# A vision-transformer block on one core, rewritten: loads by partition rows, 16-wide scores, biases off the matmuls, folded low-rank factors, halves in turn

## What is computed

```
h  = patches @ W.T + b + pos_emb                      # 512x768 @ 768x256
z  = layernorm(h);  k, q, v = split(z @ W_kqv + b_kqv)  # 256 -> 3x256, 16 heads of 16
a  = softmax(q k^T / 4 + slope_h * (j - i), causal)     # within one image: 16x16 per head
h  = h + (a v) @ W_proj + b_proj
z2 = layernorm(h)
f  = z2 @ (tern(w_fc)*s).T + gate * (z2 @ v.T @ fast_b.T @ u.T)   # 256 -> 1024, rank 16
h  = h + (relu(f)**2) @ (tern(w_mlp)*s2).T            # 1024 -> 256
# s: mean |w| of a row; tern: w/s rounded and clipped to -1, 0, 1
```

## Time and profile before

| | |
|---|---|
| median of 3 runs | 98.38 us (98.31 to 99.17) |
| the profiled execution | 99.0 us, span 97.2 us |
| PE / PEld busy | 71.5 / 57.4 us |
| DVE / ACT / POOL busy | 58.7 / 43.4 / 19.7 us |
| mean granted TensorE clock | 0.895 |

### The profile page before, as it was taken

One profiled execution on the slowest core, in us unless ns is written; L12 is line 12 of the kernel. 1 busy time (PEld: TensorE's weight loads), 2 busy tenths in 40 slices (PEclk: granted clock), 3 DMA queues, 4 the chain that ended last, 5 costly groups with the idle time before them and its releaser, 6 DMA issues.

```text
span 97.2 us, 1915 instructions
## 1 busy us (share of the span) xinstructions
PE 71.5 (74%) x776; PEld 57.4 (59%) x776; DVE 58.7 (60%) x118; ACT 43.4 (45%) x86; POOL 19.7 (20%) x21
## 2 busy tenths in 40 slices
PE   5958589899999999440000258696699999999980
PEld 4725467777777787330000247674577887888970
DVE  0300037957289799999999500228873867885590
ACT  3503003599762670619100087350223994976600
POOL 6000024089990000000199600000000000000000
PEclk9999999999999999997555555559999999999999
DMA  1899999970000000000000000000000000000015
GB/s 52 239 287 263 312 380 384 396 195 12 0 0 0 0 7 7 0 0 0 0 0 0 0 0 7 7 0 0 0 7 0 0 0 0 7 0 0 0 40 176
DMA packets 7644, 6.75 MB, mean 69 GB/s; under 512 B 2002, under 2 KB 7378, under 8 KB 7636
## 3 DMA queue, kind: packets, MB, share of 16 engines
q1 hardware_dynamic: 7056, 6.25, 19.9%
q10 hardware_dynamic: 580, 0.38, 1.7%
HBM read 6.10 MB, written 0.52 MB: 68 GB/s over the span
## 4 chain that ended last, share of the span: by engine, by line
PE 45%; DVE 23%; DMA 11%; POOL 7%; ACT 6%; issue 4%; SPq 1%; ACTq 0%; DVEq 0%
PE psum L327 14%; PE psum L488 9%; PE psum L457 8%; DMA pos_sb<-pos 8%; POOL mlp_tern L1069 6%; PE psum L415 4%; PE psum L467 3%; DMA wtok_sb<-wtok_t 3%; PE psum L340 3%; DVE shifted L913 3%; DVE smax L911 2%; ACT mlp_t L675 2%; DVE bn L851 2%; PE psum L331 2%; DVE h L849 2%
## 5 line engine op out<-in xcount | busy, mean ns | idle before, releaser
L331 PE MATMUL psum<-wtok_sb,x_sb 128*128 128x256 f32 x48 | 11.6, 388 | 3.0 <-DMA wtok_sb<-wtok_t 2.7
L331 PEld LDWEIGHTS psum<-wtok_sb,x_sb 128*128 128x128 f32 x48 | 8.6, 190 | 5.5 <-DMA wtok_sb<-wtok_t 3.7
L517 PE MATMUL psum<-ident_bf,mlp_tern 128*128 128x128 bf16 x16 | 1.9, 312 | 12.7 <-DVE mlp_tern L816 12.7
L1069 POOL TENSOR_SCALAR mlp_tern<-mlp_sb,mlp_scale 128x1024 bf16<-128x1024 f32 x2 | 5.7, 2843 | 18.9 <-DVE mlp_scale L805 18.9
L517 PEld LDWEIGHTS psum<-ident_bf,mlp_tern 128*128 128x128 bf16 x16 | 1.6, 146 | 12.9 <-DVE mlp_tern L816 12.9
L457 PE MATMUL psum<-zt_hi,fc_t 128*128 128x256 f32 x32 | 8.4, 296 | 0.0
L488 PE MATMUL psum<-sq_hi,mlp_t 128*128 128x256 f32 x32 | 8.4, 298 | 0.0
L999 DVE TENSOR_TENSOR kqv_sb<-wtok_sb 128x512 f32<-128x512 f32 x8 | 5.5, 690 | 4.7 <-PE psum L488 2.8
L457 PE MATMUL psum<-zt_lo,fc_t 128*128 128x256 f32 x32 | 7.9, 281 | 0.0
L774 ACT ACTIVATE wtok_sb<-psum,fc_scale 128x256 f32<-128x256 f32 x16 | 6.7, 468 | 2.8 <-PE psum L467 2.8
L488 PE MATMUL psum<-sq_lo,mlp_t 128*128 128x256 f32 x32 | 7.8, 281 | 0.0
(11 more groups left out here) (117 smaller groups left out, 179.0 us busy)
## 6 DMA issues: line engine op xcount, KB each, us to landing
fc_sb<-w_fc SPq DMA_DIRECT2D x1, 1024.0 KB, 11.6
mlp_sb<-w_mlp SPq DMA_DIRECT2D x1, 1024.0 KB, 8.2
x_sb<-x_t SPq DMA_DIRECT2D x2, 384.0 KB, 8.9
kqv_sb<-w_kqv SPq DMA_DIRECT2D x3, 256.0 KB, 9.5
x_sb<-x_t SPq DMA_DIRECT2D x2, 256.0 KB, 3.7
wtok_sb<-wtok_t SPq DMA_DIRECT2D x2, 256.0 KB, 5.6
out_t<-x_sb SPq DMA_DIRECT2D x4, 128.0 KB, 1.8
x_sb<-x_t SPq DMA_DIRECT2D x2, 128.0 KB, 2.4
```

The source lines that it names most:

```text
L331: return pe.matmul(tok_ps[b], x_sb[:, k, b * P:(b + 1) * P], wtok_sb[:, k, :], start=k == 0, stop=k == KF - 1)
L1069: pool.tensor_scalar(dst[:, m, :], w[:, m, :], scale[:, 2, m:m + 1], None, ALU.is_lt).then_inc(signal, 1)
```

## The change

Most of the file is rewritten. What is computed stays the same, and the last part (`hidden_main`, `hidden_low`, `mlp_out`, `squares`) keeps its products. The parts:

1. Every array is laid out by partition on the host. x and W of one 128-row chunk come as one load with 2 KB per partition (`head`), the second half of x as two loads (`tail`); positions and token bias come in one load from the SP queue, ahead of chunk 4. `fc` and `mlp` come in two loads each. All loads go through SP.
2. The bias of q, k and v is no longer a product. q's is added while it is copied out, k's in its copy, v's by POOL after a DVE transpose.
3. The scores of one image are 16 wide. q is spread with the mask into four copies (`q_spread`, 64 stationary columns) and k moves 16 columns. Softmax tiles have 512 elements per half; `prob_n` is written into a zeroed 32-wide tile so that the 32x32 transpose can be used.
4. v is computed feature-major and transposed by DVE; `values` keeps its number of products.
5. The low-rank path: `fast_b` is folded into u once, v is repeated, and `low_rank_c` with its copy is gone.
6. The fc threshold marks move from DVE to POOL. The order on each engine is new: scores of a half come right behind its q, k, v; softmax of half 0 comes ahead of the fc ternary weights; `values(0)` comes after `turn_fc`, and the mlp ternary weights and `turn_mlp` come after the second layer norm, inside the hidden layer. Standard deviations are taken per block.

```diff
 # SP
-for i, (k, n) in enumerate(CHUNKS): ... x_sb chunk; wtok_sb chunk
+for k in range(KF):
+    if k == LAST:
+        sp.dma_start(pos_sb[:, :, :], pos).then_inc(pos_in, 16)
+    sp.dma_start(head_sb[:, k, :], head[:, k, :]).then_inc(head_in[k], 16)
+# then tail 0, consts, tail 1, w_q, w_k, w_v, w_fc x2, proj_bias, u, v, fb, w_mlp x2, w_proj
 # PE
-    pairs = [(bias_parts[:, c:c + P], ones[:, :])]
+            mm = pe.matmul(ps[f][:, g * HT:(g + 1) * HT], w, part[f][:, k, :], ...)
 ...
-mm = pe.matmul(s_ps[f][j * PAIR:(j + 1) * PAIR, c:c + P],
-               q_sb[rows_, f, g, n * PAIR:(n + 1) * PAIR], k_spread[rows_, f, g, n, :, :], ...)
+for g in range(GRP):
+    for n in range(IMG_H):                      # 16 images of a half
+        t = slice(n * S, (n + 1) * S); c = (g * IMG_H + n) * S
+        for r in range(2):
+            rows = slice(r * 64, (r + 1) * 64)
+            mm = pe.matmul(s_ps[f][rows, c:c + S], q_spread[rows, f, g * IMG_H + n, :, :],
+                           k_sb[rows, f, g, t], start=False, stop=True, ...)
 ...
+for i in range(QUAD):
+    rows = slice(i * PAIR, (i + 1) * PAIR)
+    mm = pe.matmul(y_ps[f][g][rows, n * 64:(n + 1) * 64], v_turned[rows, f, g, n, :],
+                   prob_t[rows, f, 2 * p:2 * p + 2, :], start=True, stop=True)
 # PE order behind the embedding
+query(0); key(0); turn(1, z); value(0); scores(0)
+query(1); key(1); value(1); scores(1)
+fold_u(); turn_fc(); values(0); turn_u(); project(0); values(1)
+turn(0, z2); project(1); low_rank(0); hidden_main(0, 0); hidden_main(0, 1)
+hidden_low(0, 0); hidden_low(0, 1); turn_mlp(); turn(0, h2); hidden(0, 2)
+turn(1, z2); turn(1, h2); hidden(0, 3); mlp_out(0, 0); low_rank(1); mlp_out(0, 1)
+hidden(1, 0); mlp_out(0, 2); hidden(1, 1); mlp_out(0, 3); hidden(1, 2); mlp_out(1, 0)
+hidden(1, 3); mlp_out(1, 1); mlp_out(1, 2); mlp_out(1, 3)
 # ACT order
+norm_std 0, 1; weight_high(Q); zt_hi(0); weight_high(K); norm_std 2, 3; weight_high(V)
+Exp table; query_spread(0); zt_hi(1); fc_sums; query_spread(1); exponentials(0)
+mlp_sums; exponentials(1); Sqrt table; fc_t x2; odd_rows(0); u_t x2; norm_std 0, 1
+odd_rows(1); z2t_hi(0); norm_std 2; low_high(0); norm_std 3; squares(0), (1); mlp_t x2; ...
 # DVE order
+stats1(0), (1); normalise1(0), (1); bias_tables; stats1(2); zt_low(0); normalise1(2)
+stats1(3); normalise1(3); query_spread(0); key_copy(0); zt_low(1); value_turn(0)
+softmax_shift(0); query_spread(1); key_copy(1); softmax_divide(0); scales(fc)
+value_turn(1); softmax_shift(1); low_rank_factors; fc_ternaries; softmax_divide(1)
+rows_sum(0); scales(mlp); stats2(0), (1); normalise2(0), (1); rows_sum(1); z2t_low(0)
+stats2(2), (3); normalise2(2); low_low(0); normalise2(3); mlp ternary x2; squares ...
 # DVE, one of the two spreads of q
+dve.wait_ge(q_spread_act, f + 1)
+dve.scalar_tensor_tensor(q_spread[:, f, :, h, :], src, quad_mask[:, h:h + 1], bias, ALU.mult, ALU.add)
 # POOL order
+memset prob_n; posb; kqv_lo x3; residual(0); value_bias(0); residual(1); below(fc) x8
+value_bias(1); hidden_factors; value_factors; below(mlp) x2
```

More of the change, by code:

```diff
@@ L129, in build_program @@
[L129 to L142, removed]
@@ L163, in build_program @@
[L163 to L174, removed]
+        q_ps = [bank[6], bank[2]]
@@ L179, in build_program @@
-        bias_in = sem("bias_in")
+        fc_in = [sem(f"fc_in{i}") for i in range(2)]
+        mlp_in = [sem(f"mlp_in{i}") for i in range(KE)]
         small_in = sem("small_in")
@@ L421, in project @@
-            def project(f, blocks=range(BH)):
-                pe.wait_ge(proj_in, 16)
-                pe.wait_ge(yt_ready, f + 1)
-                for b in blocks:
-                    split_product(o_ps[f * BH + b], [(yt[:, f, g * BH + b, :], proj_sb[:, g, :])
-                                                     for g in range(GRP)]).then_inc(o_done, 1)
-            def low_rank_a(f):
-                pe.wait_ge(v_split, 2)
+                        mm = pe.matmul(o_ps[f * BH + b], yt[:, f, g, b * P:(b + 1) * P], proj_sb[:, g, :],
+                                       start=g == 0, stop=g == GRP - 1)
@@ new lines, in project, with fold_u, turn_u @@
+                    mm.then_inc(o_done, 1)
+            def fold_u():
+                pe.wait_ge(small_in, 48)
+                for m in range(KH):
+                    mm = pe.matmul(uf_ps[:, m * RANK:(m + 1) * RANK], u_sb[:, m * P:(m + 1) * P], fb_sb[:, :],
+                                   start=True, stop=True)
+                mm.then_inc(uf_done, 1)
+            def turn_u():
+                pe.wait_ge(u_step, 6)
+                for i in range(2):
+                    pe.wait_ge(fct_ready, i + 1)
+                    for m in range(4):
+                        mm = pe.transpose(ut_ps[i][:, m * P:(m + 1) * P],
+                                          u_fold[:, 4 * i + m, :, :, :, :].bitcast(F32), ident)
+                    mm.then_inc(ut_turned, 1)
@@ new lines, in turn_fc, with turn_mlp @@
+            def turn_fc():
+                pe.wait_ge(identbf_done, 1)
+                pe.wait_ge(fc_ternary, KH)
+                for k in range(KE):
+                    for m in range(KH):
+                        mm = pe.transpose(fct_ps[k][:, m * P:(m + 1) * P], fc_tern[:, m, k * P:(k + 1) * P],
+                                          ident_bf[:, :])
+                    mm.then_inc(fct_turned, 1)
+            def turn_mlp():
+                pe.wait_ge(mlp_ternary, KE)
+                for i in range(2):
+                    for m in range(4):
+                        for o in range(KE):
+                            c = (m * KE + o) * P
+                            mm = pe.transpose(mlpt_ps[i][:, c:c + P],
+                                              mlp_tern[:, o, (4 * i + m) * P:(4 * i + m + 1) * P], ident_bf[:, :])
+                    mm.then_inc(mlpt_turned, 1)
@@ L1005, in _ @@
+            scales(fc_sum, fc_scale, KH, E, fc_summed, fc_scaled)
+            value_turn(1)
+            softmax_shift(1)
+            low_rank_factors()
+            fc_ternaries(range(0, KH))
+            softmax_divide(1)
+            rows_sum(0)
+            scales(mlp_sum, mlp_scale, KE, HID, mlp_summed, mlp_scaled)
+            stats2(0)
+            stats2(1)
+            normalise2(0)
+            normalise2(1)
+            rows_sum(1)
+            z2t_low(0)
+            stats2(2)
             stats2(3)
-            normalise(1, 1, h2, std2, rstd2, z2_ready)
+            normalise2(2)
@@ L1007, in _ @@
             low_low(0)
+            normalise2(3)
+            ternary(mlp_sb, mlp_scale, mlp_tern, 0, mlp_cmp, mlp_ternary)
+            ternary(mlp_sb, mlp_scale, mlp_tern, 1, mlp_cmp, mlp_ternary)
             squares(0)
+            squares(1)
+            squares(2)
             z2t_low(1)
-            squares(1)
-            low_a_copy(1)
-            squares(2)
+            squares(3)
             low_low(1)
-            squares(3)
-            for n in range(PAIRS, HALVES * PAIRS):
+            for n in range(STEPS, HALVES * STEPS):
```

1004 lines of the change are left out of this document (472 added, 532 removed).

## The result

The changed kernel takes **93.96 us** (median of four runs, 93.16 to 94.5) against 98.78 us for the kernel before in the same comparison (98.31 to 99.24). The ratio is 0.9506, with a 95% interval of 0.941 to 0.9601: faster, as forecast, but by 4.8 us and not by the 13.4 that lie between the forecast of 85.0 and the 98.4 us that it starts from. The measured time is above the range of 81 to 91.

The account below looks back on a forecast made before the run. Bound by when the last, PE-bound stage can start and its length: `low_rank(0)` at 54.2 instead of 71.08 us, plus 26.6, last product at 80.8, 2.8 behind it, span 83.6, so 85 us; range 81 to 91.

Parts of the forecast that it names:

- The wait for `mlp_tern`: In the hidden layer, PE idles 2.2 us because DVE finishes the mlp ternaries only at 59.7 us.
- the last stage: From `low_rank(0)` to the last product: 23.3 us as before, plus 2.2 idle and 1.1 for `turn_mlp`, 26.6 us.
- The rival in which small matmuls lose their concurrency: Scores and values: row groups sharing one bank run singly at 58 ns, 21 us more, 106 us; chance 0.05.
- q, k, v, scores: Stage after the embedding: scores of a half take 2.4 us, those of half 1 end at 34.7 instead of 39.1 us.
- score instructions at 18 ns: Sign the forecast is right: each of a half's 128 score instructions on PE takes 18 ns.
- scores over 5 us: Sign the forecast is wrong: a run of score or values instructions on PE takes over 5 us.
- the clock stays low: Rival: between 42 us and the hidden layer PE's clock holds at 1.2 GHz, +4 us, 89 us; chance 0.2.
- POOL's marks run at a quarter of 2.84 us each: fc threshold marks on POOL: eight at 0.71 us, 5.7 us in all, from 35.7 to 41.4 us.
- Both ends meet: fc weights: POOL's marks end at 41.4 and DVE's ternaries at 41.7 us, so moving the marks costs PE nothing.
- The first add: DVE's first add in the embedding comes at 8.8 us instead of 13.73; past 10.5 would show the forecast wrong.
- the 13.7 us that it sets against 512 x 27 ns: Gain that lost concurrency of small matmuls would eat, deciding from 45 ns per instruction.
- its five chances: Lost concurrency 0.05, low clock 0.2, loads at 241 GB/s 0.1, shorter than forecast 0.07, the forecast itself 0.58.

Follow-up runs that it names:

- experiment 2: The changed kernel with the upper row group's scores written to a second PSUM bank that nobody reads: 94.79 us (one run).
- experiment 5: The changed kernel with DVE's fc scales moved ahead of the softmax of half 0, so POOL's fc marks start sooner: 93.29 us, ratio 0.9317.
- experiment 6: As experiment 5, with the eight fc ternaries also moved ahead of the spread of q of half 1 on DVE: 90.09 us, ratio 0.9108.
- experiment 11: The changed kernel with `bias_tables` moved behind `zt_low(0)` on DVE: 94.09 us, ratio 0.9409.
- experiment 4: The changed kernel with all score matmuls of the lower row group first, then all of the upper, instead of alternating: 105.44 us (one run).
- experiment 1: The changed kernel with 18 dummy products on PE in its wait ahead of the scores of half 0: 91.74 us, ratio 0.928.
- experiment 3: The changed kernel with 32 stationary columns instead of 64 per score matmul, half of the scores left out: 91.87 us (one run).
- experiment 7: experiment 1 and experiment 6 together on the changed kernel, fc ternaries split three and five around `softmax_divide(0)`: 88.68 us.
- experiment 8: The changed kernel with 20 dummy products in PE's wait for `mlp_tern`: 93.11 us, ratio 0.9403.

## Why the prediction was wrong, step by step

**Right.** The direction and its mechanism, as far as the traces show it: the mlp weights no longer stand ahead of `low_rank(0)`, which starts at 63.18 instead of 71.08 us. No run puts one part of the change back, so how the 4.8 us divide among its parts is not shown. Groups of six products without the bias take 0.70 us at full clock (forecast 0.75). The wait for `mlp_tern` is 2.3 us (2.2). That the last stage took 26.0 us (26.6) is in part luck: it holds the third hollow, of about 1 us, which the forecast did not have, and without it the same products take 25.1 (experiments 2, 5, 6 and 11), 1.5 less than forecast. The values keep their pitch, a softmax pass over half the elements takes 0.69 (0.65), and `turn_fc` does run at 1.2 GHz, 1.86 us (1.9). The rival in which small matmuls lose their concurrency is refuted by experiments 2 and 4.

**Wrong: the step "q, k, v, scores".** It took 18 ns for an instruction of a form that the trace did not have. I bounded it by 2.0 and 14.7 us for a half and chose near the low end because row groups still alternate. They do, but the earlier trace rows had shown 32 stationary columns, and the change has 64. Measured: 3.91 us at 2.4 GHz for 2.4 (experiments 1 and 3). On the path that is 1.5 us for scores(0); scores(1) lie beside DVE's work. The forecast itself named the point that would show this ("score instructions at 18 ns"), and its first sign of being wrong, scores over 5 us, came true with 6.09.

By the Trainium skill (TensorE: Matmul & The Clock Gate, "LDWEIGHTS (loading the stationary operand)") a weight load costs by its columns and not by its contraction rows. The 17.2 and 30.5 ns agree with it in direction as to the columns; the contraction rows were 64 in both. The floor of about 25 ns between starts that the Trainium skill gives (TensorE: Matmul & The Clock Gate, "Wait — 56ns, not 53.3ns?"), and which the forecast set against the trace, is contradicted twice more, by 17.2 ns and by 15.5 ns, both in alternating row groups.

**Wrong: the same step's clock.** It let the clock fall only in PE's wait for the fc weights. It fell at 26.0 as well, with PE busy on score instructions. Price: 6.09 - 3.91 = 2.2 us in scores(0), and the spread of half 1 was done 6.9 us after scores(0) instead of 5.5, 1.4 more (the twelve products of query(1) alone took 2.87 us, where 1.4 is their time at full clock). Together with the pitch and the late start (0.4) this is the 5.5 us at the spread of half 1: 0.4 + 1.5 + 2.2 + 1.4. The rival "the clock stays low" had the right mechanism and the wrong place: I looked for it only behind 42 us, where the earlier trace rows had shown it, and priced it at 4 us there.

**Wrong: "POOL's marks run at a quarter of 2.84 us each".** They take 0.92 in experiment 5 and 0.99 here, beside DVE's ternaries: 7.8 us for 5.7, all on the path, because DVE paces behind the last mark. With DVE's last ternary at 0.87 instead of 0.42 this is 2.55 of the 2.7 us added between 41.3 and 50. "Both ends meet" was also too smooth: when POOL starts sooner (experiments 1 and 5), `fold_u` holds DVE up instead.

**Missed, but covered.** `fold_u` stands in the forecast only as u factors of 0.6 us on DVE. Its 8 products, recorded as 16 instructions, take 2.68 us: the first eight instructions, at 2.4 GHz, start 0.12 us apart, and from 43.0 on the clock is low. Wholly at 1.2 GHz they take 3.59 us (224 ns each). In the changed kernel's profile DVE waits 1.2 us for it and POOL's marks still end later; in the profiles of experiments 1, 5, 6, 7, 8 and 11, where the clock fell before or at its start, DVE waits 1.9 to 2.4 us for it. The first add was 1.2 us late, and that was the loads and the start, not the pitch of the embedding. PE began at 4.00 instead of 3.6 and waited three times for the next load (engine line waited for: us in total, times, longest):

```profile
PEld psum L303 <- DMA head_sb<-head: 1.1, 3, 0.4
```

Without these waits its 24 instructions take (6.77 - 1.1) / 24 = 0.236 us each, as forecast. The loads came at 306 and 282 GB/s (2.4 to 5 and 5 to 7 us), between the two rates of the earlier trace rows. 0.4 us of this reach the scores.

**Sum.** +5.5 to the spread of half 1, +0.1 to the scales, +2.7 to `fc_tern`, +0.7 to `low_rank(0)` (values(0) took 2.60 us for 2.0 at the low clock), -0.65 in the last stage: 8.35 us of the last product's time. Two slips of the forecast change none of this: the 13.7 us that it sets against 512 x 27 ns should be 13.4, and its five chances leave nothing over for the 0.01 of no change.

**Open.** How the clock's part and the order's part add up: experiments 1 and 6 gain 2.2 and 3.9 us by their medians and 5.3 together (7.2 by the one run of 86.8), but runs of one kernel lie 1 to 2 us apart, and where the hollows begin differs between profiles of code that is the same up to there (the first at 25.1, 26.0 or 27.4). Why it differs stays open. The two `q_bias_m` instructions of 64 elements take 1.31 and 0.24 us; what the first spends its time on was not settled.

## What to carry to other kernels

A pitch belongs to a form: before taking a duration from the trace for a matmul with wider stationary operand, or for an elementwise operation of a quarter of the width, ask which dimension the nearest row fixes, and put the forecast between that row and the next one rather than on it. When a change puts many small matmuls after a wait, forecast the clock from there on, as a range, since here small matmuls did not keep it up, and what pays for a fall is the dense work behind it. Before a hollow in the clock row is said to be cured, look whether it also goes away in profiles that leave its cause in place: the third one here did. When weights are prepared on DVE, put them in the stretch in which DVE waits for PE: moving them from one busy place to another gained nothing (experiment 11), while moving them into a wait gained 3.9 us (experiment 6).

## What the hardware showed

- The granted clock fell to 1.2 GHz with PE busy: at 26.0 after 1.2 us of score instructions behind an idle stretch of 1.8, and at 43.0 after 5 us of scores and small products. Eighteen 128x256 products in the idle stretch moved the first fall to 37.5, 27.8, 29.2 and 36.9 in four profiles. The fall at 70.3 came in some profiles and not in others, with the same 2.3 us of idle time ahead of it.
- 128 fp32 matmul instructions (64 products) with 16 moving columns in alternating row groups: 17.2 ns each with 32 stationary columns, 30.5 with 64, both at 2.4 GHz; 59 ns with 64 columns at the same clock when the row groups do not alternate.
- The shared bank cost nothing (29.5 ns with two banks, 30.5 with one, both at 2.4 GHz). The Trainium skill (TensorEngine Tiling (Array Packing), "Gotcha 1: PSUM Pressure") says that row tiles cannot use one bank at the same time; for row groups that write different partitions these runs show no such hold-up.
- POOL's compare with a scalar per partition: 0.92 us for 256 columns and 2.84 for 1024. A straight line through the two leaves about 0.28 us that does not depend on the width, which is an estimate.
